# A chain of four adapted linear layers on one Trainium2 core: the first weight delta from 64 rows of LoRA factors instead of 128 rows padded with zeros

## The reference

```python
x = x + _L0_cond_ref(x, L0_cond_W, L0_cond_b, condB_coeff, mask)          # x [8, 256, 1024]
x = x + _L1_cond_ref(x, L1_cond_weight, L1_cond_scale_log, condB_codebook, L1_cond_lora_A, L1_cond_lora_B)
x = x + _L2_cond_ref(x, itok_B_0_23, L2_cond_W, L2_cond_b, L2_cond_lora_As, L2_cond_lora_Bs)
x = x + _L3_cond_ref(x, L3_cond_A, L3_cond_B, itok_B_4_50)
```

```python
lora_delta = lora_B @ lora_A * (32.0 / 64)            # [1024, 64] @ [64, 1024]
normalized = (weight + lora_delta).reshape(O, 8, 128) / exp(scale_log)
quantized = cb[searchsorted(thresholds, normalized)]  # 8 levels of the normalized codebook
w_eff = (quantized * scale).reshape(O, I) + lora_delta
return x @ w_eff.T
```

## Time and profile before

| | us |
|---|---|
| median of 3 runs | 550.1 (549.83 to 550.27) |
| the profiled execution | 549.03 |
| its span, first to last instruction | 547.4 |
| PE busy in the span | 531.3 |
| DVE busy | 461.2 |
| ACT busy | 350.7 |
| DMA queue of SP, share of 16 engines | 52.1% |

### The profile page before, as it was taken

The page is one execution under the profiler, slowest core; times in us unless marked ns, Lnnn a source line. Parts: engine busy times, 40 slices in busy tenths (PEclk is TensorE's granted clock), DMA queues, the critical chain, the costliest instruction groups (busy, mean ns, idle before and its releaser), DMA issues.

```text
span 547.4 us, 9005 instructions
## 1 busy us (share of the span) xinstructions
PE 531.3 (97%) x2864; PEld 458.2 (84%) x2864; DVE 461.2 (84%) x742; ACT 350.7 (64%) x681; POOL 169.0 (31%) x170
## 2 busy tenths in 40 slices
PE   4899999999999999999999999999999999999997
PEld 4898788888888788888888888888888888888886
DVE  5997898988865879987999889897897987989853
ACT  3776775776745774675767657666676665766730
POOL 2669767987734320003004003000300400400120
PEclk9999999999999999999999999999999999999999
DMA  8767031833395993458446455746845645564222
GB/s 228 247 86 152 24 117 43 255 128 125 89 208 167 356 333 61 151 185 173 131 141 188 92 179 168 124 151 193 160 135 152 175 101 182 169 108 154 77 50 77
DMA packets 147281, 82.57 MB, mean 151 GB/s; under 512 B 105060, under 2 KB 124516, under 8 KB 147124
## 3 DMA queue, kind: packets, MB, share of 16 engines
q1 hardware_dynamic: 145444, 78.34, 52.1%
q0 software_dynamic: 1520, 3.86, 2.7%
q10 hardware_dynamic: 288, 0.01, 0.0%
HBM read 65.93 MB, written 16.26 MB: 150 GB/s over the span
## 4 chain that ended last, share of the span: by engine, by line
PE 75%; DVE 11%; DMA 4%; ACT 4%; SPq 3%; issue 2%; DVEq 0%; ACTq 0%
PE bank L1679 17%; PE bank L1686 9%; PE bank L1723 5%; PE bank L1722 5%; PE bank L1553 5%; PE bank L1721 5%; PE bank L1555 5%; PE bank L1554 5%; PE bank L1772 3%; PE bank L1770 3%; PE bank L1771 3%; DVE merged_ring L1207 3%; PE bank L1734 2%; DVE m_lo L1213 2%; PE bank L1463 2%; DMA mask_ring<-in_mask_Bx4096x_ik 2%
## 5 line engine op out<-in xcount | busy, mean ns | idle before, releaser
L1679 PE MATMUL bank<-x_t_pair,m_hi 128*128 128x512 f32 x512 | 128.8, 394 | 1.9 <-ACT m_hi L820 1.7
L605 POOL TENSOR_TENSOR x_t_pair<-x_sum,x_t_pair 128x256 fp32r<-128x256 f32 x32 | 29.8, 959 | 290.9 <-ACT x_t_pair L893 290.9
L1679 PEld LDWEIGHTS bank<-x_t_pair,m_hi 128*128 128x128 f32 x512 | 92.6, 189 | 19.9 <-ACT m_hi L820 3.1
L820 ACT CAST m_hi<-merged_ring 128x512 fp32r<-128x512 f32 x128 | 73.0, 619 | 51.0 <-PE bank L1686 25.7
L810 ACT ACTIVATE merged_ring<-mask_ring,batch_now 128x1024 f32<-128x1024 int32 x64 | 78.1, 1243 | 25.1 <-DMA mask_ring<-in_mask_Bx4096x_ik 24.3
L1213 DVE TENSOR_TENSOR m_lo<-merged_ring,m_hi 128x512 fp32r<-128x512 f32 x128 | 84.6, 709 | 9.1 <-ACT m_hi L820 9.0
L1207 DVE TENSOR_TENSOR merged_ring<-merged_ring,w_t 128x1024 f32<-128x1024 f32 x64 | 76.4, 1221 | 14.3 <-ACT merged_ring L810 13.3
L1686 PEld LDWEIGHTS bank<-x_t_pair,m_lo 128*128 128x128 f32 x512 | 69.9, 191 | 5.0
L1686 PE MATMUL bank<-x_t_pair,m_lo 128*128 128x256 f32 x512 | 71.5, 283 | 0.0
L1723 PE MATMUL bank<-P_hi,x_t_pair 128*128 128x496 f32 x160 | 61.5, 385 | 0.0
L1722 PE MATMUL bank<-P_lo,x_t_pair 128*128 128x496 f32 x160 | 61.5, 384 | 0.0
(11 more groups left out here) (221 smaller groups left out, 1110.2 us busy)
## 6 DMA issues: line engine op xcount, KB each, us to landing
mask_ring<-in_mask_Bx4096x_ik SPq DMA_DIRECT2D x64, 512.0 KB, 4.4
w_nat<-in_L_cond_W SPq DMA_DIRECT2D x14, 512.0 KB, 5.1
x_t_squares<-in_x SPq DMA_DIRECT2D x56, 128.0 KB, 3.0
w_raw<-in_L_cond_weight SPq DMA_DIRECT2D x16, 256.0 KB, 4.8
out<-out_staged SPq DMA_DIRECT2D x16, 248.0 KB, 5.5
w0t_dram<-w_out SPq DMA_DIRECT2D x14, 256.0 KB, 2.7
w_t<-w0t_dram SPq DMA_DIRECT2D x6, 512.0 KB, 5.0
g_batch<-g_dram POOLq DMA_DIRECT2D x21, 128.0 KB, 4.2
```

Source lines behind the costliest of these rows:

```text
L820: nc.scalar.copy(Mh[:, n % MR], ring_f[:, k % MR, h * HALF:(h + 1) * HALF]).then_inc(s["h_set"], 1)
L1679: mm(bank[L0_BANK[HT * h + j]][:, :], Mh[:, n % MR, j * P:(j + 1) * P], xThl[:, :, :, k + i, :], start=(k + i == 0), stop=False, skip_grou ...
```

## The change

The two factors now lie twice or side by side in the 128 partitions. `la` holds lora_A in rows 0 to 63 and again in rows 64 to 127, by a second DMA of 256 KB. `lbt` holds lora_B's first 512 rows, transposed, in rows 0 to 63 and the last 512 in rows 64 to 127; it is 512 wide instead of 1024. For that lora_B is loaded by two DMAs of 128 KB into a tile in which the two halves lie beside each other, PE transposes it in four steps of 128 columns instead of eight of 64, and ACT copies it once. A delta of half h multiplies 64 rows with 64 rows, the lower ones for h = 0 and the upper ones for h = 1. The deltas 0 and 1 are issued alternately, one product of each in turn, and so are 2 and 3; delta 3 thereby moves from behind `v_part(7)` to behind `v_part(4)`, where the pair waits for `eff_set` of half 0, which delta 2 alone did not. Deltas 4 to 15 keep their places. The two memsets and their semaphore are gone.

```diff
-            sp.dma_start(lbn[:, :, :], lora_b.rearrange("(t p) r -> p t r", p=P)).then_inc(s["lora_b_in"], 16)
+            for h in range(2):
+                sp.dma_start(lbn[:, :, h], lora_b.rearrange("(h t p) r -> h p t r", h=2, p=P)[h]).then_inc(s["lora_b_in"], 16)
             sp.dma_start(la[0:RL, :], lora_a).then_inc(s["lora_a_in"], 16)
             sp.dma_start(cb[:, :], row(codebook).broadcast_to([P, NCB])).then_inc(s["cb_in"], 16)
             sp.dma_start(sc[:, :, :], scale_log.rearrange("(t p) g o -> p t (g o)", p=P)).then_inc(s["sc_in"], 16)
+            sp.dma_start(la[RL:2 * RL, :], lora_a).then_inc(s["lora_a_in"], 16)
...
-            for h in range(2):
-                act.wait_ge(s["lbt_tr"], h + 1)
-                nc.scalar.mul(lbt[0:RL, h * 512:(h + 1) * 512], bank[5 + h][0:RL, :], L1_SCALE).then_inc(s["lbt_set"], 1)
+            act.wait_ge(s["lbt_tr"], 1)
+            nc.scalar.mul(lbt[:, :], bank[5][:, :], L1_SCALE).then_inc(s["lbt_set"], 1)
...
-            nc.vector.memset(la[RL:P, :], 0.0).then_inc(s["lora_pad"], 1)
-            nc.vector.memset(lbt[RL:P, :], 0.0).then_inc(s["lora_pad"], 1)
...
-            pe.wait_ge(s["lora_b_in"], 16)
-            for h in range(2):
+            pe.wait_ge(s["lora_b_in"], 32)
+            for t in range(HT):
+                ins = nc.tensor.transpose(bank[5][:, t * P:(t + 1) * P], lbn[:, t].rearrange("p h r -> p (h r)"), ident[:, :])
+            ins.then_inc(s["lbt_tr"], 1)
+
+            def delta_half(n, t):
+                q, rows = n // 2, slice(n % 2 * RL, (n % 2 + 1) * RL)
+                return mm(dps(n)[:, t * P:(t + 1) * P], lbt[rows, t * P:(t + 1) * P], la[rows, q * P:(q + 1) * P],
+                          start=(t == 0), stop=True, skip_group_check=True)
+
+            def delta(n):
+                if n >= 3:
+
+                    pe.wait_ge(s["eff_set"], n - 2)
                 for t in range(HT):
-                    ins = nc.tensor.transpose(bank[5 + h][0:RL, t * P:(t + 1) * P], lbn[:, h * HT + t, :], ident[:, :])
-                ins.then_inc(s["lbt_tr"], 1)
...
+                    ins = delta_half(n, t)
+                ins.then_inc(s["delta_done"], 1)
+
+            def delta_pair(q):
+                if q == 0:
+                    pe.wait_ge(s["lbt_set"], 1)
+                else:
+                    pe.wait_ge(s["eff_set"], 2 * q - 1)
                 for t in range(HT):
-                    k = h * HT + t
-
-                    ins = mm(dps(n)[:, t * P:(t + 1) * P], lbt[:, k * P:(k + 1) * P], la[:, q * P:(q + 1) * P],
-                             start=(t == 0), stop=True, skip_group_check=True)
-                ins.then_inc(s["delta_done"], 1)
+                    for h in range(2):
+                        ins = delta_half(2 * q + h, t)
+                        if t == HT - 1:
+                            ins.then_inc(s["delta_done"], 1)
...
-            pe.wait_ge(s["lora_pad"], 2)
-            pe.wait_ge(s["lora_a_in"], 16)
-            delta(0)
-            delta(1)
+            pe.wait_ge(s["lora_a_in"], 32)
+            delta_pair(0)
...
-            delta(2)
+            delta_pair(1)
...
-            delta(3)
```

More of the change, by code:

```diff
@@ L107, in cond_resid_chain @@
     a2n = at("a2_nat", [P, KT, NB, R], F32, lo + 4 * KB)
-    lbn = at("lb_nat", [P, KT, RL], F32, lo + 28 * KB)
+    lbn = at("lb_nat", [P, HT, 2, RL], F32, lo + 28 * KB)
     own = at("own_batch", [P, NB, R], F32, reg_z3 + 20 * KB)
@@ L167, in cond_resid_chain @@
     c_sum = at("c_sum", [P, HW], F32, reg_la + 2 * KB)
-    lbt = at("lora_b_t", [P, D], F32, reg_b2)
+    lbt = at("lora_b_t", [P, HALF], F32, reg_b2)
     off = [reg_c]
@@ L222, in cond_resid_chain @@
             s_set v_set h_set m_ready m_used l0_done x1_part x1_sum x1_hi x1_ready0 x1_ready1 x_turned xt_hi xt_first xt_later xt_ready u_done u_part u_summed u_hi u_ready
-            out_done out_added out_st0 out_st1 out_st2 out_st3 c_in gl_in c_stored lora_pad now_set coef_now
+            out_done out_added out_st0 out_st1 out_st2 out_st3 c_in gl_in c_stored now_set coef_now
             t_step t_summed t_hi t_ready a_summed a_hi a_ready prod_done c_sums c11_set out_copied b2_split side_set side_done side_step side_st""".split()}
@@ L1445, in _ @@
             pe.wait_ge(s["ident_set"], 1)
-            pe.wait_ge(s["lora_b_in"], 16)
-            for h in range(2):
-                for t in range(HT):
-                    ins = nc.tensor.transpose(bank[5 + h][0:RL, t * P:(t + 1) * P], lbn[:, h * HT + t, :], ident[:, :])
-                ins.then_inc(s["lbt_tr"], 1)
+            pe.wait_ge(s["lora_b_in"], 32)
[6 more added lines that the diff above has]
+                          start=(t == 0), stop=True, skip_group_check=True)
             def delta(n):
-                q, h = n // 2, n % 2
                 if n >= 3:
                     pe.wait_ge(s["eff_set"], n - 2)
-                elif n == 0:
-                    pe.wait_ge(s["lbt_set"], 2)
                 for t in range(HT):
-                    k = h * HT + t
-                    ins = mm(dps(n)[:, t * P:(t + 1) * P], lbt[:, k * P:(k + 1) * P], la[:, q * P:(q + 1) * P],
-                             start=(t == 0), stop=True, skip_group_check=True)
+                    ins = delta_half(n, t)
                 ins.then_inc(s["delta_done"], 1)
+            def delta_pair(q):
[3 more added lines that the diff above has]
+                    pe.wait_ge(s["eff_set"], 2 * q - 1)
+                for t in range(HT):
+                    for h in range(2):
+                        ins = delta_half(2 * q + h, t)
+                        if t == HT - 1:
+                            ins.then_inc(s["delta_done"], 1)
             def w0_transpose(blk, h):
```

## The result

The changed kernel takes 553.3 us (median of 6 runs, 552.66 to 553.94) against 550.18 (6 runs, 548.73 to 550.83) for the kernel before: a ratio of 1.0059, 95% interval 1.0044 to 1.0075. That is 3.1 us slower; 552.8 had been forecast. A second set of runs of both kernels gave 552.49 against 548.92, 1.0066 (1.0054 to 1.0078). The profiled execution took 553.82 us, its span is 551.9.

The account below looks back on a forecast made before the run. PE was taken as the bound, busy 531.3 of 547.4 us, but before 62 us a chain through `norm(1)`. 1.8 + 0.9 + 0 = 2.7 us on the profiled 549.03 gave 551.7, plus 1.1 for the median 552.8; range 549.9 to 555.2.

Parts of the forecast that it names:

- the head: Before PE's dense stretch at 62 us: PE's pace stays at 1.2 GHz past b3's landing, delaying `norm(1)` by 1.8 us.
- the switches: PE's dense stretch, nine deltas: 18 changes between 128-row and 64-row products at 0.05 us each, 0.9 us in all.
- the other bound: Dense stretch: an emptied array at each of 18 row changes, 0.16 us each, thus 2.9 us.
- the rival of the emptied array: Dense stretch: every switch empties the array, 2.9 us, with `norm(1)` 0.3 to 1.8 late: 553.3 to 554.8, chance 0.15.
- a shift of `norm(1)` comes through whole: ACT's `norm(1)` at 21.00: any delay of it reaches 62.4 us, and so the end, at full size.
- What was costed at nothing: Memsets 0; transposes and ACT copy hidden by lora_A's second copy; deltas 2 and 3 with their wait 0; raw weight's landing hidden.
- The serial rival: First pair of deltas isn't concurrent, running 9.15 to 12.95, so the first term starts 1.5 us late: 552.5, chance 0.12.
- The faster rival: Dense stretch: 64-row products take half of 0.111 us, nine deltas save 4.0 us: 546.4 to 547.9, chance 0.09.

Follow-up runs that it names:

- late_full: The changed kernel with deltas 4 to 15 over 128 rows again, the two pairs at the head still on 64: 550.0 us, ratio 1.0012 to the kernel before.
- late_64_only: The kernel before with deltas 4 to 15 multiplying rows 0 to 63 only, nothing else changed: 552.54 us, ratio 1.006.
- twice: The changed kernel with each of the deltas 4 to 15 issued twice in a row: 562.09 us, ratio 1.0233 to the kernel before.
- split_only: The kernel before with lora_B loaded by two DMAs of 128 KB instead of one of 256 KB: 549.32 us, ratio 1.0007.
- warm_head: The changed kernel with idle products of the identity in PE's gaps before about 15 us: 552.15 us, ratio 1.0059 to the kernel before.
- serial_lines: The changed kernel with pairs issued delta by delta, each delta on its own source line: 553.57 us, a single run.

## Why the prediction was right, and where it was not

The time, the sign and the range held: 553.3 against a forecast of 552.8. But it holds as a sum of two terms that were both off, 1.3 us too much at the head and 1.8 too little at the switches, so that the nearness of the number is luck; and one of the rivals describes the kernel better than the forecast does.

- **The switches** were the term that was mis-sized. I took 0.05 us for each, 0.9 in all, by its nearness to a row in which a switch of columns cost nothing. They cost about 0.15, 2.7 us in all: the other bound, 0.16, was near the true size. That is the price of the rival of the emptied array. late_full, late_64_only and twice show the price and its place by three different edits; that the array is emptied is not shown, and what the traces do show is that the first weight load behind a switch no longer runs ahead. The step that failed was to take a switch of columns as near kin to a switch of rows, against a reason that I had written down myself; that reason, how far results travel in the array, no run measures either. The Trainium skill (TensorEngine Tiling (Array Packing), Key Properties) says that changing the tiling mode drains TensorE. The trace agrees for rows in that a switch has a price, 0.15 us; for the matmul with 32 columns it shows none, and its weight load at 264.15 runs 0.21 us ahead.
- **The head** was put at 1.8 us and measured 0.4 to 0.5 in the traces; by the times, 0.5 to 0.9 are left of the loss beside the 2.7. Its mechanism stood in the changed kernel's trace: the pair started at 9.02 (9.15 forecast) and took 2.08 us (2.1), it was nearly worthless, the transposes of b3 ran at half pace, and `w2_lo(1)` carried the delay to `norm(1)`. Two sizes were off. b3 came at 14.65, not 15.4, since the tokens were there 1.9 us earlier, which split_only shows to be the work of lora_B's two DMAs; I had seen only the 256 KB more. That is 0.75 of the 0.9 us by which `norm(1)` came earlier than forecast. And the price "a shift of `norm(1)` comes through whole" was wrong. In the changed kernel 0.87 us were still 0.80 when SP issued group 2's raw weight (45.77 against 44.97) and 0.53 when it had landed, since the load took 4.64 us instead of 4.91; from there on 0.54 came through. SP's own way there isn't rigid either: in late_full `norm(1)` starts at 21.75 and that load at 44.96. In warm_head 1.1 became at most 0.6, because a second chain through POOL and ACT lies just below the one through SP.
- **What was costed at nothing** was nothing: the memsets, the transposes and the copy, deltas 2 and 3 with their new wait (PE goes from `v_part(4)` into the pair without a gap), the raw weight's later landing.
- **The serial rival** (the pair isn't concurrent) is out for the changed kernel: 2.08 us for the pair, not 3.8. Even issued delta by delta it took 3.09.
- **The faster rival** is out: a 64-row product takes as long as a 128-row one, 0.89 us for the eight further instructions of twice.

## What to carry to other kernels

In this kernel padding a short contraction with zeros costs nothing in a stream of full matmuls, and taking the padding away costs two switches for each island of short ones: 0.3 us on a delta of 0.89. Short matmuls pay only where upper and lower rows have work together, and only if what waits for them had been waiting; here nobody was. A shift at the head isn't worth its own size without a look at what else comes just as late. And to price an edit in one stretch, compare the length of that stretch between two points of the trace: it repeats within 0.05 us here, but for one late load, while its start differs by 0.8 between two kernels with the same head.

## What the runs showed of the hardware that was not expected

Behind a switch between 128-row and 64-row matmuls the first weight load doesn't run ahead of its matmul (70.89 and 70.90), where in a stream of one kind it runs 0.22 us ahead (70.06 and 70.28). Matmuls on rows 64 to 127 started ahead of up to three matmuls on rows 0 to 63 that stand earlier in the program (serial_lines, one trace). The Trainium skill (TensorE: Matmul & The Clock Gate, Part 3: Packing small matmuls) says that matmuls keep the order of the program in start and end. The trace disagrees for the starts (10.38 ahead of 10.58, 10.80 and 11.01). Loading lora_B by two DMAs of 128 KB instead of one of 256 KB brought a small transfer on another queue, the tokens, 1.9 us earlier (4.44 against 6.39 us). And traces of programs that differ by 14 idle matmuls at the head differed by 2 us some 80 us later, through one load that took 6.8 us instead of 4.3; the cause is open, and it is as large as most effects looked for here.
